# Products that nobody reads, placed on the matrix engine in seven idle stretches of a fused two-layer decoder

## Chip, cores and metric

The kernel runs on one core of a Trainium2 chip. The metric is the time on the device in microseconds, from one launch of the whole program. Lower is better. The engines are called PE (TensorE, PEld for its weight loads), DVE (VectorE), ACT (ScalarE), POOL (GpSimd) and SP (the queue that issues the DMAs).

## What is computed

Two decoder layers on `x` of 16 sequences x 128 positions x 128 features. Each of the six sublayers is added to `x`, and each reads a layer norm of it; the program counts the layer norms from 0, the text from the first.

```python
x = x + mamba(layernorm(x))                    # 1st norm: W_in, delta, B, C, a scan over 128 positions, W_out
x = x + cross_attention(layernorm(x), ctx)     # 2nd norm: one head, 120 context rows of 64
x = x + experts(layernorm(x))                  # 3rd norm: 8 experts, top 2, and a shared one
x = x + reflected_lru(layernorm(x))            # 4th norm: the recurrence below
x = x + heads_attention(layernorm(x), ctx)     # 5th norm: 16 heads of 8
x = x + selu_experts(layernorm(x))             # 6th norm: 8 experts, top 2, hidden 512

def step(h_prev, x_t, v_t, lam_t):             # of reflected_lru, 127 times
    Qh = h_prev - 2.0 * v_t * (sum(v_t * h_prev) / sum(v_t * v_t))
    return lam_t * Qh + (1.0 - lam_t) * x_t
```

All experts are computed for all positions and weighed afterwards, so the shapes are fixed.

## The kernel before

It is written engine by engine: each engine has one program, and semaphores named in `S` order them. The 16 sequences are handled in four groups (`NG` = 4) of four (`GB` = 4), so most products have 128 x 512 outputs, one bank of PSUM. TensorE takes its instructions strictly in the order of its program, so a wait in it holds back all that stands behind. `bank(n)` is PSUM bank n, and `mm` is a matrix product; `mm(out, ident, y)` copies y.

A layer norm for group g goes round the engines. VectorE computes the statistics (L812 to L818), GpSimd the inverse deviation (L319, L320), ScalarE normalizes the first two sequences (L507, semaphore `ln_xn_a`) and VectorE the other two (L824, `ln_xn_b`). TensorE transposes the four (`transpose_xn`, L1338), ScalarE copies them out of PSUM (`copy_xnT`, L510 to L518, semaphore `ln_xnT`), and VectorE keeps what is lost in the shorter type (`ln_lower`, L827 to L834, `ln_lo`). The projections behind it are `up` (L1352, three products for one output, line L1356) and `down` (L1345, line L1349).

The places that the change touches, in order of time:

- The first norm and `W_in`. TensorE waits for `const`, set by GpSimd when the identity is built (L327 to L329), transposes group 0, then per group transposes the next one and makes four `up` outputs. ScalarE applies silu to them (L544); before that it loads a table.
- The fourth norm: three transposed groups, then `xz(0)` (12 products of L1356), the fourth group, `xz(1)`, and the products with `Wl` and `Wv` (L1569).
- `chunk_dots` and `solve`: TensorE's dot products in groups, with which VectorE solves for chunks of four positions (`u_done`, `c_done`, L1100 to L1122). The third and the fourth group's `solve` come after TensorE's last dot product.
- The rounds: 32 chunks (`NC`) one after the other. A round is a chain between VectorE (L1183 to L1199) and TensorE: `s_known` (L1629) puts known sums in PSUM, and a product with ones (L1639) adds what depends on the last round. In each round but the last stand two products with the identity into bank 5 that nobody reads (L1643). VectorE handles finished spans between (`piece`, L1143).
- After the last round VectorE, ScalarE and GpSimd finish the last span and the gate (`gated`), and TensorE waits for it and makes the output projection with `down`.
- The fifth norm: TensorE makes the keys of all groups (L1653), then per group the transposes (L1342) and the values (L1659, which wait for VectorE's `hk_lo`), then the queries (L1664) with a bias row of 128 x 128 (L1666). ScalarE takes them in the order normalize, key copy, copy of the group before, value copy of the group before (`keys_and_values`, L589).
- The attention with 16 heads: a loop over 16 sequences. `head_scores` (L1675, on 32 rows each), `head_transposes` (L1685), `head_values` (L1696), `head_sums` (L1704), `head_out` (L1710) on TensorE. VectorE takes the maximum and subtracts it (L1233, L1236) and divides (L1241), ScalarE takes exponentials and copies (L766, L771), GpSimd spreads keys and values (L460, L477). The first scores stand ahead of a wait for all queries (`hq_lo`).

Of the kernel before, what the change touches and what calls it, by code (L numbers as in the profile page):

```python
# [12 lines left out]
P = 128  # L13
B, T, D = 16, 128, 128
N = B * T
GB = 4
NG = B // GB
# [29 lines left out]
def decoder_program(nc, a, out):  # L47

    with ExitStack() as ctx:
# [1285 lines left out]
        def _(pe):  # L1335
            mm = nc.tensor.matmul

            def transpose_xn(i, g):  # L1338
                for b in range(GB):
                    if b % (GB // 2) == 0:  # L1340
                        pe.wait_ge(S["ln_xn_b" if b else "ln_xn_a"], i * NG + g + 1)
                    ins = nc.tensor.transpose(bank(ln_bank(i, g))[:, 0, b * T:(b + 1) * T], xn[:, g * GB + b, :], ident[:])  # L1342
                ins.then_inc(S["ln_tr"], 1)
# [15 lines left out]
            pe.wait_ge(S["const"], 1)  # L1359

            transpose_xn(0, 0)
            for g in range(NG):
                if g + 1 < NG:
                    transpose_xn(0, g + 1)
                pe.wait_ge(S["w_split"], 1)
                pe.wait_ge(S["ln_lo"], g + 1)
                for m in range(4):
                    if g:
                        pe.wait_ge(S["in_silu"], 4 * g - 3 + m)
                    up(bank(4 + m)[:, 0, :], 0, m, g).then_inc(S["in_mm"], 1)  # L1370
# [177 lines left out]

            for g in range(NG - 1):
                transpose_xn(3, g)  # L1550
            pe.wait_ge(S["w_lru"], 16 * 6)
# [74 lines left out]
            def s_known(c):  # L1626
                if c >= 2:
                    pe.wait_ge(S["s_copied"], c - 1)
                mm(slot(c), ident[:], cp.rearrange("p (q k) -> p q k", k=KG)[:, :, GB * c:GB * c + GB], start=True, stop=False,  # L1629
                   skip_group_check=True)  # L1630

            pe.wait_ge(S["vv_read"], NG)
            pe.wait_ge(S["l_ev"], HI * NG)
# [3 lines left out]
            for c in range(NC):  # L1637
                pe.wait_ge(S["r_sum"], c + 1)
                mm(slot(c), ones[:], us[:, c % 2], start=False, stop=True, skip_group_check=True).then_inc(S["s_mm"], 1)  # L1639
                if c + 1 < NC:  # L1640
                    s_known(c + 1)
                    for k in range(2):
                        mm(bank(5)[:, 0, 0:256], ident[:], cp[:, 0:256], start=True, stop=True)  # L1643
            pe.wait_ge(S["z_silu"], 2 * HI)
            pe.wait_ge(S["s_copied"], NC)
# [9 lines left out]
            for g in range(NG):  # L1655
                transpose_xn(4, g)
                pe.wait_ge(S["hk_lo"], g + 1)
                for b in range(GB):
                    ins = mm(bank(4 + g)[0:LK, 0, b * D:(b + 1) * D], w["ctxT"][:, g * GB + b, :], w["Wv1"][:], start=True, stop=True)  # L1659
                ins.then_inc(S["hv_mm"], 1)  # L1660
            for g in range(NG):
                pe.wait_ge(S["hv_ev"], g + 1)
# [51 lines left out]
            head_scores(0, 1)  # L1714
            pe.wait_ge(S["hq_lo"], NG)
            for b in range(B + 2):
                if b + 1 < B:
# [123 lines left out]
```

## Time and profile before

| | |
|---|---|
| median of 3 runs | 1047.51 us (1047.32 to 1052.38) |
| the profiled execution, whole | 1046.03 us |
| its span, first to last instruction | 1044.3 us |
| mean granted clock of TensorE | 0.958 |
| PE / PEld busy | 903.1 / 665.5 us (86% / 64%) |
| DVE / ACT / POOL busy | 811.1 / 544.6 / 420.2 us |
| chain that ended last | PE 52%, DVE 17%, ACT 5%, issue 3%, POOL 1% |

The granted clock is a share of TensorE's full 2.4 GHz; it has two levels here, 1.00 and 0.50. The first record of it stands at 15.4 us, and the views print 1.00 ahead of it, where nothing was recorded. Shares of busy time are means over stages with different limits, so a stage is read by its own rows. In a row of the timeline stand: start, length, engine and line, operation, tiles, shapes, count, and in brackets how long the engine was idle before it and what released it. A row may merge several instructions, and its length then reaches from the first to the last. A few records of matrix products can be missing.

### The profile page before, as it was taken

How to read it: one execution, taken by the hardware profiler on the slowest of the kernel's cores; microseconds unless marked ns; L12 is line 12 of the kernel's file. 1: busy time of each engine (PE TensorE's matmuls, PEld its weight loads, DVE VectorE, ACT ScalarE, POOL GpSimd, SP SyncE). 2: the span in 40 equal slices, each digit the busy share in tenths (PEclk: the TensorE clock that was granted, in tenths of full speed). 3: DMA queues.
4: the chain of work that ended last, by engine and by line, in shares of the span. 5: the costliest groups of instructions: out<-in, count | busy, mean ns of one | idle time of the engine just before them, and what ended most of it. 6: DMA issues, size and time to landing. Idle time of an engine off the chain costs nothing.

```text
span 1044.3 us, 15167 instructions
## 1 busy us (share of the span) xinstructions
PE 903.1 (86%) x5628; PEld 665.5 (64%) x5628; DVE 811.1 (78%) x1450; ACT 544.6 (52%) x979; POOL 420.2 (40%) x400
## 2 busy tenths in 40 slices
PE   6967877778899999989885767899968999999997
PEld 4432222223688888866654546576646789999997
DVE  6799999999767555573897886599975588878886
ACT  6456566654653222236533223466645467677775
POOL 6479999999200101112982354544420001011110
PEclk9979999999999999999987997599999999999999
DMA  6000000000001001000000001000000000000001
GB/s 186 1 0 1 0 1 0 0 1 1 1 2 31 16 16 31 16 1 1 1 0 1 1 1 41 1 2 2 2 1 1 1 21 21 6 16 21 21 21 41
DMA packets 19860, 13.82 MB, mean 13 GB/s; under 512 B 3067, under 2 KB 18313, under 8 KB 19786
## 3 DMA queue, kind: packets, MB, share of 16 engines
q1 hardware_dynamic: 19786, 12.84, 4.4%
q8 instruction: 45, 0.74, 0.3%
q14 instruction: 29, 0.24, 0.1%
HBM read 11.79 MB, written 1.05 MB: 12 GB/s over the span
## 4 chain that ended last, share of the span: by engine, by line
PE 52%; DVE 17%; ACT 5%; issue 3%; POOL 1%; DVEq 0%; ACTq 0%; POOLq 0%
PE ps L1356 19%; PE ps L1349 17%; PE ps L1569 3%; DVE small L1233 2%; PE ps L1743 2%; DVE G L1236 2%; PE ps L1685 1%; PE ps L1639 1%; PE ps L1400 1%; DVE R L1194 1%; DVE stats L812 1%; DVE ps L1199 1%; PE ps L1675 1%; DVE ps L1183 1%; DVE R L1185 1%
## 5 line engine op out<-in xcount | busy, mean ns | idle before, releaser
L1356 PE MATMUL ps<-xhl,whl 128*128 128x512 f32 x960 | 247.3, 407 | 12.7 <-DVE xhl L834 5.1
L1356 PEld LDWEIGHTS ps<-xhl,whl 128*128 128x128 f32 x960 | 179.1, 194 | 52.3 <-issue 13.4
L784 ACT ACTIVATE G<-ps,w_exp_bi 128x512 f32<-128x512 f32 x128 | 89.9, 702 | 65.9 <-PE ps L1356 54.9
L1349 PEld LDWEIGHTS ps<-R,G 128*128 128x128 f32 x1024 | 119.0, 192 | 6.4 <-DVE G L1279 4.1
L1349 PE MATMUL ps<-R,G 128*128 128x128 f32 x1024 | 119.7, 275 | 3.1 <-DVE G L1279 3.1
L356 POOL TENSOR_TENSOR R<-G,R 128x1024 f32<-128x1024 f32 x43 | 100.5, 2352 | 19.4 <-ACT R L550 15.8
L942 DVE TENSOR_TENSOR_SCAN R<-ps,R 128x1024 f32<-128x1024 f32 x43 | 97.6, 2279 | 5.7 <-POOL R L365 5.7
L785 ACT ACTIVATE G<-ps,ebs 128x512 f32<-128x512 f32 x144 | 102.0, 708 | 0.0
L649 ACT ACTIVATE G<-ps 128x512 f32<-128x512 f32 x72 | 42.8, 597 | 112.8 <-PE ps L1356 112.8
L1039 DVE SCALAR_TENSOR_TENSOR X<-ps,cw,X 128x128 f32<-128x128 f32 x272 | 76.5, 344 | 23.4 <-PE ps L1349 23.2
L1279 DVE SCALAR_TENSOR_TENSOR G<-G 128x1024 f32<-128x1024 f32 x72 | 91.6, 1272 | 2.5
L1278 DVE TENSOR_SCALAR G<-G 128x1024 f32<-128x1024 f32 x72 | 55.2, 767 | 47.6 <-ACT G L785 47.2
L1379 PE MATMUL ps<-bc,sel 96*128 96x512 bf16 x128 | 46.8, 394 | 49.8 <-ACT LN L557 22.1
L324 POOL CAST whl<-R 128x512 fp32r<-128x512 f32 x8 | 6.5, 819 | 195.0 <-DMA R<-in_exp_wo_dram 162.8
L577 ACT ACTIVATE ps<-G,negA 128x508 f32<-128x508 f32 x128 | 83.3, 689 | 3.0 <-DVE R L942 2.9
L1048 DVE TENSOR_TENSOR G<-G,ps 128x512 f32<-128x512 f32 x72 | 49.0, 687 | 44.5 <-ACT G L649 44.5
L1400 PE MATMUL ps<-R,ident 128*128 128x512 f32 x172 | 82.0, 599 | 0.0
L550 ACT COPY R<-ps 128x512 f32<-128x512 f32 x64 | 37.4, 585 | 77.7 <-PE ps L1379 77.7
L1379 PEld LDWEIGHTS ps<-bc,sel 96*128 96x128 bf16 x128 | 12.5, 98 | 102.3 <-ACT LN L557 35.8
L1349 PEld LDWEIGHTS ps<-ew,G 128*128 128x128 f32 x576 | 69.6, 191 | 2.8 <-DVE G L1048 0.3
L1349 PE MATMUL ps<-ew,G 128*128 128x128 f32 x576 | 70.2, 275 | 0.1
L319 POOL TENSOR_TENSOR rstd<-small,mhalf 128x4 f32<-128x4 f32 x24 | 24.7, 1028 | 83.9 <-DVE small L818 83.9
(270 smaller groups left out, 1726.2 us busy)
## 6 DMA issues: line engine op xcount, KB each, us to landing
ew<-in_w_dram SPq DMA_DIRECT2D x24, 128.0 KB, 2.2
R<-in_exp_wi_dram SPq DMA_DIRECT2D x8, 256.0 KB, 2.7
R<-in_exp_wo_dram SPq DMA_DIRECT2D x8, 256.0 KB, 3.2
X<-in_x_dram SPq DMA_DIRECT2D x4, 256.0 KB, 3.9
out_dram<-X SPq DMA_DIRECT2D x4, 256.0 KB, 2.3
w_ctxT<-in_ctxT_dram SPq DMA_DIRECT2D x1, 487.5 KB
ew<-in_sw_dram SPq DMA_DIRECT2D x3, 128.0 KB, 2.5
w_W_in<-in_W_in_dram SPq DMA_DIRECT2D x1, 256.0 KB, 3.0
```

The lines of the kernel that those rows point to most:

```text
L356: gp.tensor_tensor(halves(dBu[i % 3]), duT[:, :, gcols(i // NS)], Bsb[:, i % 4:i % 4 + 1, :].broadcast_to([P, HI, GT]), ALU.mult).then_inc ...
L577: sc.activation(bank(2 * j + m)[:, 0, :].rearrange("p (b t) -> p b t", b=GB)[:, :, 1:T], dT[:, m, gcols(g)].rearrange("p (b t) -> p b t", ...
L784: sc.activation(G[:, 0, slot, m * GT:(m + 1) * GT], banks[:, m, :], ACT.Exp, bias=exp_bias[m])
L785: sc.activation(G[:, 1, slot, m * GT:(m + 1) * GT], banks[:, m, :], ACT.Relu, bias=lin_bias[m], scale=SELU_L).then_inc(S[act_s], 1)
L942: v.tensor_tensor_scan(hst[i % 3], bank(2 * j, 2).rearrange("p h n -> p (h n)"), dBu[i % 3], 0.0, ALU.mult, ALU.add).then_inc(S["scanned"], 1)
L1039: ins = v.scalar_tensor_tensor(X[:, bi, :], bank(4 + i % 2)[:, 0, b * D:(b + 1) * D], cw[:, bi, e:e + 1], X[:, bi, :], ALU.mult, ALU.add)
L1278: step(v.tensor_scalar(G[:, 0, slot, half], G[:, 0, slot, half], 1.0, 1.0, ALU.min, ALU.subtract))
L1279: ins = v.scalar_tensor_tensor(G[:, 2, slot, half], G[:, 0, slot, half], SELU_LA, G[:, 1, slot, half], ALU.mult, ALU.add)
L1349: ins = mm(bank(o)[:, 0, b * width:(b + 1) * width], lhs(k, b), rhs(k), start=k == 0, stop=k == ks - 1)
L1356: ins = mm(mix(out) if n == N_WIN1 else out, whl[:, wslot(n), i, m * P:(m + 1) * P], rhs, start=k == 0, stop=k == 2)
L1379: mm(bank(bank_i)[:, 0, :], sel[:, r, :], bc3[:, gcols(g)], start=True, stop=True).then_inc(S[s], 1)
L1400: ins = mm(bank(6 + m)[:, 0, :], ident[:], hC[i % 3][:, m * GT:(m + 1) * GT], start=False, stop=i % NS == NS - 1, skip_group_check=True)
```

## The change

TensorE's program gets a helper, `unread(o, n)`: n products of the identity with itself, 128 x 128 in float32, into the first quarter of PSUM bank o. Nobody reads them, and no semaphore is set by them. 115 of them are placed: 18, 5 and 3 in the first norm; 5, 3 and 7 in the fourth; 14 ahead of the rounds; 34 behind them; 6 behind the values of each of the first three groups in the fifth norm; 8 behind the first scores of the attention. The 14 stand behind three new waits (for all but the last group's `solve` and copy), because bank 5 is in use till then; the 6 stand behind a new wait for the copy of group 0, because bank 0 holds its transposes. No other engine's program changes.

```diff
+            def unread(o, n):
+
+                for _ in range(n):
+                    mm(bank(o)[:, 0, 0:P], ident[:], ident[:], start=True, stop=True)
+
-            def transpose_xn(i, g):
+            def transpose_xn(i, g, between=0):
                 for b in range(GB):
+                    if b == GB // 2:
+                        unread(7, between)
                     if b % (GB // 2) == 0:
                         pe.wait_ge(S["ln_xn_b" if b else "ln_xn_a"], i * NG + g + 1)
...
             pe.wait_ge(S["const"], 1)
 
+            unread(7, 18)
             transpose_xn(0, 0)
+            unread(7, 5)
             for g in range(NG):
                 if g + 1 < NG:
                     transpose_xn(0, g + 1)
+                if g == 0:
+                    unread(7, 3)
...
-            for g in range(NG - 1):
-                transpose_xn(3, g)
+            transpose_xn(3, 0)
+            transpose_xn(3, 1)
+            unread(7, 5)
+            transpose_xn(3, 2, between=3)
+            unread(7, 7)
...
+            pe.wait_ge(S["u_done"], 3 * (NG - 1))
+            pe.wait_ge(S["c_done"], 2 * (NG - 1))
+            pe.wait_ge(S["e_ev"], NG - 1)
+            unread(5, 14)
             pe.wait_ge(S["vv_read"], NG)
...
+            unread(5, 34)
             pe.wait_ge(S["z_silu"], 2 * HI)
             pe.wait_ge(S["s_copied"], NC)
...
                 ins.then_inc(S["hv_mm"], 1)
+                if g + 1 < NG:
+                    pe.wait_ge(S["ln_xnT"], 4 * NG + 1)
+                    unread(0, 6)
...
             head_scores(0, 0)
             head_scores(0, 1)
             pe.wait_ge(S["hq_lo"], NG)
+            unread(7, 8)
```

## Rows read from the trace of the kernel before

**Rows 1.** The page, TensorE's granted clock in 40 equal slices, in tenths.
```profile
PEclk9979999999999999999987997599999999999999
```

**Rows 2.** Stretches: start and end, length, busy time of five engines, clock, DMA.
```profile
465.90:472.70 6.80, 5.40 (x13) 4.17 (x14) 2.34 (x5) 2.67 (x6) 0.00 (x0) 0.50 0.00 1
...
551.30:564.90 13.60, 6.69 (x23) 5.82 (x23) 10.16 (x29) 4.07 (x10) 0.00 (x0) 0.50 0.00 0
...
565.00:623.00 58.00, 45.17 (x229) 32.03 (x228) 48.93 (x168) 14.61 (x64) 24.41 (x30) 1.00 0.00 1
...
632.30:636.50 4.20, 4.19 (x19) 4.20 (x20) 0.40 (x1) 0.00 (x0) 0.00 (x0) 0.50 0.00 0
636.70:650.20 13.50, 12.09 (x86) 9.87 (x85) 12.18 (x55) 6.91 (x16) 6.16 (x14) 1.00 0.29 80
650.30:660.40 10.10, 10.10 (x26) 5.99 (x26) 2.16 (x3) 4.52 (x9) 5.71 (x3) 0.50 0.00 0
660.60:663.80 3.20, 1.43 (x14) 0.52 (x12) 2.60 (x4) 2.05 (x3) 3.20 (x8) 1.00 0.00 0
663.90:677.50 13.60, 12.39 (x76) 8.88 (x78) 10.10 (x9) 5.93 (x9) 4.78 (x12) 0.50 0.00 1
677.70:765.00 87.30, 80.82 (x1263) 60.61 (x1260) 81.48 (x125) 54.32 (x84) 37.02 (x84) 1.00 0.01 2
```

**Rows 3.** The timeline at the start, all engines.
```profile
1.41 0.29 POOL L329 TENSOR_SCALAR_AFFINE_SELECT ident<-ident 128x128 f32<-128x128 f32 x1 [0.24 <-POOL ident L328]
...
9.29 0.56 ACT L518 CAST xhl<-ps 128x512 fp32r<-128x512 f32 x1
...
10.89 5.07 PE L1356 MATMUL ps<-xhl,whl 128*128 128x512 f32 x12 [0.34 <-DVE xhl L834]
...
14.90 1.28 ACT L544 ACT_TABLE_LOAD   x1
```

**Rows 4.** The chain that ended last: start, length, engine and line, count.
```profile
452.15 1.78 PE ps L1349 x16
...
467.30 5.46 PE ps L1356 x12
473.27 2.74 PE ps L1356 x12
...
632.31 3.77 PE ps L1349 x16
```

**Rows 5.** The timeline in the fourth norm and around the rounds.
```profile
463.64 0.44 PE L1342 MATMUL ps<-ident,LN 128*128 128x128 f32 x2 [1.36 <-ACT LN L507]
...
464.98 0.44 PE L1342 MATMUL ps<-ident,LN 128*128 128x128 f32 x2 [0.90 <-DVE LN L824]
...
552.11 0.28 DVE L1122 TENSOR_TENSOR R<-R,ps 128x128 f32<-128x128 f32 x1
...
558.00 0.66 PE L1629 MATMUL ps<-R,ident 128*128 128x64 f32 x2 [9.74 <-DVE R L1122]
...
623.14 0.43 PE L1639 MATMUL ps<-R,ones 128*128 128x64 f32 x2 [0.46 <-DVE R L1185]
```

**Rows 6.** VectorE's timeline in the rounds, one instruction of each.
```profile
558.73 0.20 DVE L1188 TENSOR_TENSOR R<-LN,ps 128x32 f32<-128x32 f32 x1
...
566.07 0.20 DVE L1188 TENSOR_TENSOR R<-LN,ps 128x32 f32<-128x32 f32 x1
568.03 0.20 DVE L1188 TENSOR_TENSOR R<-LN,ps 128x32 f32<-128x32 f32 x1
```

**Rows 7.** The timeline of the queries in the fifth norm.
```profile
653.61 1.92 PE L1664 MATMUL ps<-LN,w_Wq 128*128 128x512 f32 x2
...
656.17 4.98 PE L1664 MATMUL ps<-LN,w_Wq 128*128 128x512 f32 x6
```

**Rows 8.** What VectorE waited for from 661 to 684 us: in total, times, longest.
```profile
DVE G L1241 <- PE ps L1704: 3.4, 1, 3.4
DVE small L1233 <- PE ps L1675: 1.8, 2, 1.2
```

## The prediction

> **What bounds the kernel now.** I read the slices of the page first, for TensorE's granted clock: in most of the span it is full, and it dips in slices 3, 21, 22, 25 and 26 [rows 1]. Then the table of stretches, cut where the clock changes. The reader is to see five long stretches at 0.50, which is 1.2 of the 2.4 GHz, and what TensorE did in and before them [rows 2]: 465.9 to 472.7 us (fourth layer norm), 551.3 to 564.9 (into the rounds), 632.3 to 636.5 (output projection behind the rounds), 650.3 to 660.4 and 663.9 to 677.5 (fifth layer norm, first turns of attention). In the last one TensorE is busy for 12.39 of 13.6 us, so there it works at half speed and others wait for it. Third, the chain that ended last, for the price: twelve `up` products take 5.46 us at the low clock and 2.74 at the full one, sixteen instructions of `down` 3.77 against 1.78 [rows 4]. All four low pieces that the sum uses lie on that chain. So the kernel is bound by TensorE or VectorE by turns, and a few microseconds are lost wherever TensorE comes back from a pause.
>
> **Price of one product.** A plain float32 product is recorded as two MATMULs: `down` with four batches and two halves is eight products and stands as x16 [rows 4]. With 128 columns one MATMUL is 1.78/16 = 0.111 us at full clock and 3.77/16 = 0.236 at the low one, so a product is 0.22 or 0.47 us. The change adds 115 of them, 230 MATMULs, 25.6 us at full clock. Nothing reads them; they cost only where they still run when the next needed instruction is ready.
>
> **Start (26 products).** TensorE may begin when the identity is built, at 1.41 + 0.29 = 1.7 us [rows 3]. The clock is low there: twelve `up` products take 5.07 us at 10.89 [rows 3], like the 5.46 above, though no fall is printed. 36 MATMULs at 0.236 would end at 10.2. But dense work raises the clock: it rose 4.3 us after 632.3, and 5.5 after 467.3 [rows 2, 4]. Here that is 6.0 to 7.2 us; by then 18 to 23 are done and the rest take 2.0 to 1.4 us, so they end near 8.0 to 8.6. With the four transposes (0.111 us each) behind them that is 8.5 to 9.1, and ScalarE, busy till then, takes the copy that reads them only at 9.29 [rows 3]. The next 5 and 3 products (1.1 and 0.7 us) fit between the groups at full clock. Does the faster first projection pay? It ends about 2.3 us sooner, but ScalarE's table load ends at 14.90 + 1.28 = 16.2 [rows 3] and the silus that release the next group wait for that. So I take 0. Bounds: a gain of 0.3 if ScalarE's order loosens, and 1.2 lost if the longer pause before 16.9 lets the clock fall again under the second group (half of its 2.7 us, more than ScalarE can hide).
>
> **Fourth layer norm (5, 3 and 7).** Between the transposes and the projection the engine pauses; the last one is released by VectorE's split, and the projection starts at 467.30 [rows 4]. The products are 1.1, 0.7 and 1.6 us; the gaps that they stand in are 1.36 us ahead of the third group's first half and 0.90 ahead of its second, then 467.30 - 465.42 = 1.88 ahead of the projection [rows 4, 5]. All fit at full clock, and it is full until 465.9 [rows 2]. With them the engine is busy for most of these 5 us, so the clock should stay up: 5.46 - 2.74 = 2.7 us gained [rows 4]. Next behind it is TensorE's own second projection, so the gain goes through. Bounds 0 and 2.9.
>
> **Before the rounds (14).** The new waits (third group solved) end with the `c_done` instruction at 552.11 + 0.28 = 552.4 [rows 5]; they are weaker than the waits behind them, so nothing else is held. TensorE has by then been idle since 558.00 - 9.74 = 548.3 and the clock is low from 551.3 [rows 2, 5]. 28 MATMULs at 0.236 are 6.6 us, to 559.0, against the first needed product at 558.00 [rows 5]; with the rise 4.3 to 5.5 us after their start they end at 557.7 to 558.5. So they hold the start back by 0 to 0.5 us (1.0 at worst), but the rounds run at full clock from the first. The first three rounds took 566.07 - 558.73 = 7.34 us, the next 1.96 [rows 6]: 7.34 - 3 x 1.96 = 1.46. I take 1.2 gained; bounds 1.0 lost and 1.5 gained.
>
> **After the rounds (34).** TensorE ends its last needed product at 623.14 + 0.43 = 623.6 [rows 5] at full clock, and `down` starts at 632.31 [rows 4]: a gap of 8.7 us. 68 x 0.111 = 7.5 us, to 631.1. The margin is 1.2 us, ten MATMULs at the low clock. Then the first group of `down` takes 1.78 instead of 3.77 us, and VectorE's residual and statistics wait for exactly that group: 2.0 gained, bounds 7.3 lost (see the rivals) and 2.3 gained.
>
> **Fifth layer norm (3 x 6).** Each call waits for ScalarE's copy of the first group and then runs 12 MATMULs, 1.3 us. Behind them on the queue stand the next transposes and values products, for which ScalarE waits. Together 4.0 us; in 636.7 to 650.2 TensorE is idle for 13.50 - 12.09 = 1.4 [rows 2], so the work is pushed 2.6 us later. The low clock of 650.3 to 653.6 gives back half of 3.3, so the queries start 0.9 late. They (with the bias row) took from 653.61 to 656.17 + 4.98 = 661.15 [rows 7], 7.5 us at the low clock, and at the full one half: 3.8. Net 2.8 earlier. Bounds: 2.6 lost if the clock stays low here, 3.5 gained.
>
> **Attention's first turn (8).** 16 MATMULs, 1.8 us, wait for VectorE's last lower part of the queries, with which a pause opens: TensorE was busy for 1.43 of 3.2 us in 660.6 to 663.8 [rows 2]. They fill the pause and no more. Between 661 and 684 VectorE waits 3.4 and 1.8 us for TensorE's sums and scores [rows 8]. In 677.7 to 765 VectorE is busy for 81.48 of 87.3 us [rows 2], so it sets the pace once the clock is up, and what is gained at the entry stays. These 5.2 us go at full clock; I take 4.7, since small waits remain. Bounds 0 and 5.7.
> The rule that speaks against this place: the first turns consist of transposes and of scores on 32 rows. In 677.7 to 765 the turns consist of them too, with values and sums between, and the clock is 1.00; but in 663.9 to 677.5 it stayed at 0.50 although TensorE was busy nine tenths of the time [rows 2]. The Trainium skill, TensorE: Matmul & The Clock Gate, Part 4: PE-mode transpose, says that a transpose doesn't count as busy in the way that other matmuls do. By it the sum would be 4.7 us smaller, since the clock would fall again behind the eight products; it is a rival below.
>
> **Sum.** 0 + 2.7 + 1.2 + 2.0 + 2.8 + 4.7 = 13.4 us. The profiled execution took 1046.0 us (span 1044.3 and 1.7 around it), so it would be 1032.6. The median of the runs is 1047.5, 1.5 above; against it 1034.1. I predict 1034. Where the clock falls will differ between executions by a few microseconds (the three runs reach from 1047.3 to 1052.4), so single dips may move.
>
> **The rivals.**
> 1. The clock falls again in attention's first turns. For it: the 663.9 row, the narrow scores. Against: TensorE is full-clock in all later turns, made of the same instructions, and eight full-width products stand right ahead. It gives 1034 + 4.7 = 1039. Chance 0.20.
> 2. The dips only move, or what is gained in the layer norms is given back behind the added wait of the fifth one and at the start (2.6 and 1.2 lost, no gain in the queries and attention): 1047.5 - 2.7 - 1.2 - 2.0 + 2.6 + 1.2 = 1045. For it: 4.0 us of products stand ahead of needed transposes there. Chance 0.09.
> 3. Slower: the 34 products run at the low clock. If a product of the identity with itself holds the clock no better than a pause, the clock falls a few us into the gap. All 68 at 0.236 are 16.0 us against a gap of 8.7, 7.3 late; more than ten at the low clock are enough for a loss. The fifth layer norm's 36 MATMULs at 0.236 are 8.5 us against 1.4 of idle, 7.1 more. No gain is left, and this gives 1047.5 + 7.3 + 7.1 = 1062. Against: the spare products of the rounds also multiply by the identity, and with them the clock is 1.00 through 565 to 623, where TensorE is busy for 45.17 of 58 us [rows 2]. Chance 0.04.
> 4. The products do all that is said in the layer norms and after the rounds, but VectorE absorbs less than I think in attention and half of that gain goes: 1034 + 2.4 = 1036. It lies in the forecast's own range.
>
> **How the numbers follow.** Forecast 0.67 (1030 to 1038, with rival 4), rival 1 0.20 (1037 to 1041), rival 2 0.09, rival 3 0.04. The range from 1030 to 1042 holds the first two and a little of rival 2. A measurement of this kernel can tell about 0.5% from no change, which is 1042.3 and 1052.7. Faster by more: 0.67 + 0.20 + 0.01 = 0.88; within: 0.08; slower: 0.04.
>
> **What would show it.** In the profile after: `up` at the fourth layer norm's end near 2.75 us; three first rounds at 1.96 each; the first sixteen `down` MATMULs at 1.8 us and starting when the gate releases them, not later; the queries' eight MATMULs at 3.4 us; VectorE's waits for sums and scores in the first turns gone; no clock of 0.50 between 558 and 765. The mean granted clock should go from 0.958 to about 0.98. Wrong would be a `down` that starts behind the spare products, transposes of the first layer norm's first group that end after 9.3 us, or a low clock under attention's first turns.

## The result and the profile after

The changed kernel took 1035.14 us (median of 4 runs, 1033.03 to 1037.51) against 1048.04 for the kernel before (4 runs, 1047.32 to 1052.38): ratio 0.9858, 95% interval 0.983 to 0.9885. On the chip of the last experiments it took 1038.83 (6 runs) against 1048.38: 0.9909, 0.9889 to 0.9929. Both belong to the result; of the 3.7 us between them the profiles show 2.3, which the experiments trace to one place, and the rest is open. Every ratio in this document is against the kernel before on the same chip in the same set of runs, and leaves out one execution of 3184.89 us, at a clock of 1.00, of the kernel with 68 products below, which no trace explains.

| | before | after |
|---|---|---|
| profiled execution, whole | 1046.03 us | 1035.33 us |
| its span | 1044.3 us | 1033.6 us |
| mean granted clock | 0.958 | 0.975 |
| TensorE busy, instructions | 903.1 us | 917.7 us, x5858 |

The clock in 40 slices of the span, to be held against [rows 1]:

```profile
PEclk9989999999999999999988999999998999999999
```

Slices 21 and 22 still dip, and so does slice 31, but the deep dips of 25 and 26 are gone. The table of stretches of after, in the columns of [rows 2], cut where its own clock changes:

```profile
18.40:21.80 3.40, 3.40 (x9) 2.65 (x9) 0.93 (x3) 2.75 (x6) 3.25 (x2) 0.50 0.81 240
467.10:470.10 3.00, 2.96 (x14) 2.44 (x15) 0.98 (x2) 1.76 (x3) 0.00 (x0) 1.00 0.01 3
486.10:489.50 3.40, 3.40 (x5) 1.34 (x5) 3.30 (x4) 1.87 (x4) 3.04 (x3) 0.50 0.00 0
499.70:503.10 3.40, 3.40 (x11) 2.29 (x10) 3.22 (x3) 1.65 (x4) 3.32 (x5) 0.50 0.00 0
550.90:557.70 6.80, 5.38 (x25) 5.41 (x26) 6.51 (x14) 3.40 (x6) 0.12 (x1) 0.50 0.00 0
...
630.70:645.00 14.30, 14.30 (x106) 12.46 (x107) 11.48 (x54) 5.56 (x12) 5.37 (x9) 1.00 0.25 74
650.50:656.30 5.80, 5.16 (x25) 2.14 (x23) 3.01 (x5) 4.28 (x7) 3.91 (x1) 1.00 0.00 0
656.30:667.50 11.20, 9.85 (x104) 7.43 (x108) 11.03 (x10) 6.88 (x11) 8.24 (x20) 1.00 0.01 1
```

From 557.8 to 772.7 us no clock of 0.50 is left. But there are three falls that the kernel before did not have, at 18.4, 486.1 and 499.7 us, and in the sixth norm a second one at 779.6. Now TensorE's timeline at the places of the products (L1341 is the spare product; L1349 the transposes, L1356 `down`, L1363 `up`, L1686 the queries, L1697 the scores):

```profile
1.76 5.71 PE L1341 MATMUL ps<-ident 128*128 128x128 f32 x36 [1.76 <-POOL ident L329]
7.77 0.44 PE L1349 MATMUL ps<-ident,LN 128*128 128x128 f32 x2 [0.29 <-ACT LN L507]
8.93 0.44 PE L1349 MATMUL ps<-ident,LN 128*128 128x128 f32 x2 [0.72 <-DVE LN L824]
...
18.24 4.57 PE L1363 MATMUL ps<-xhl,whl 128*128 128x512 f32 x12 [2.63 <-ACT G L544]
...
465.08 1.73 PE L1341 MATMUL ps<-ident 128*128 128x128 f32 x14
467.14 2.99 PE L1363 MATMUL ps<-xhl,whl 128*128 128x512 f32 x12 [0.33 <-DVE xhl L832]
...
552.32 5.95 PE L1341 MATMUL ps<-ident 128*128 128x128 f32 x28 [4.21 <-DVE G L1120]
558.10 0.33 PE L1643 MATMUL ps<-R,ident 128*128 128x64 f32 x2
...
621.78 7.81 PE L1341 MATMUL ps<-ident 128*128 128x128 f32 x68
...
650.58 1.02 PE L1686 MATMUL ps<-LN,w_Wq 128*128 128x512 f32 x2
...
651.94 2.84 PE L1686 MATMUL ps<-LN,w_Wq 128*128 128x512 f32 x6
...
656.35 2.05 PE L1341 MATMUL ps<-ident 128*128 128x128 f32 x16 [0.69 <-DVE qhl L1225]
658.96 0.92 PE L1697 MATMUL ps<-kz,qhl 32*128 32x480 f32 x6 [0.56 <-POOL kz L460]
```

The 68 MATMULs behind the rounds take 7.81 us and end at 629.6, a microsecond ahead of `down`. The six last of the queries take 2.84 us against 4.98 in [rows 7]. What VectorE waits for from 648 to 671 us, for [rows 8]:

```profile
DVE qhl L1225 <- ACT qhl L757: 5.0, 1, 5.0
DVE G L1241 <- PE ps L1726: 0.8, 1, 0.8
```

The 3.4 and 1.8 us for sums and scores have become 0.8. Next behind TensorE at this place is GpSimd, which spreads keys and values. These pieces of the chain that ended last, between the queries and the first turn, are now its:

```profile
652.39 4.53 POOL X L470
656.92 1.90 POOL kz L460 x2
658.83 0.14 issue
658.96 0.92 PE ps L1697 x6
```

The two profiles are compared by the start of the same VectorE instruction at the end of each stage. Each number is microseconds gained in the stage (minus: lost). "The rest" is what lies between the first scan and 464 us, and behind 679 us. The last column is a second profile of the same changed kernel, taken with the last experiments.

| stage, up to | predicted | after | after, again |
|---|---|---|---|
| start, to the first scan (56 us) | 0 | 0.28 | -2.01 |
| fourth norm, to its last split (474 us) | 2.7 | 2.5 | 2.5 |
| its recurrence, to the first round (559 us) | 0 | -2.5 | -2.4 |
| entry to the rounds (566 us) | 1.2 | 1.45 | 1.44 |
| behind the rounds, fifth norm, queries (662 us) | 2.0 + 2.8 | 4.75 | 4.74 |
| attention's first turn (679 us) | 4.7 | 4.57 | 4.55 |
| the rest | 0 | -0.3 | -0.3 |
| sum | 13.4 | 10.7 | 8.4 |

In the first profile five of the stages with a price came out within 0.3 us. What is missing is the fourth norm's gain, given back in the stage behind it, and in the second profile 2 us at the start.

### The profile page after: what moved, and what is told of

The parts are those of the page before. It is cut to its first block, busy times and chain, and to the rows that moved or that the text cites. A ratio compares the mean times of both kernels' runs of the same rounds, so it can differ in the third digit from the quotient of the medians.

```text
span 1033.6 us, 15627 instructions
## 1 busy us (share of the span) xinstructions
PE 917.7 (89%) x5858; PEld 683.8 (66%) x5858; DVE 806.5 (78%) x1450; ACT 545.2 (53%) x979; POOL 419.5 (41%) x400
## 4 chain that ended last, share of the span: by engine, by line
PE 54%; DVE 15%; ACT 4%; issue 3%; POOL 2%; DVEq 0%; ACTq 0%; POOLq 0%
PE ps L1363 20%; PE ps L1356 18%; PE ps L1583 3%; DVE small L1233 2%; PE ps L1766 2%; DVE G L1236 2%; PE ps L1411 1%; PE ps L1657 1%; DVE R L1194 1%; PE ps L1707 1%; DVE ps L1199 1%; DVE ps L1183 1%; DVE R L1185 1%; PE ps L1697 1%; DVE stats L812 1%
## 5 line engine op out<-in xcount | busy, mean ns | idle before, releaser
L1363 PE MATMUL ps<-xhl,whl 128*128 128x512 f32 x960 | 245.9, 406 | 12.6 <-DVE xhl L834 4.8
L1363 PEld LDWEIGHTS ps<-xhl,whl 128*128 128x128 f32 x960 | 178.7, 193 | 50.9 <-issue 14.3
L1356 PEld LDWEIGHTS ps<-R,G 128*128 128x128 f32 x1024 | 119.0, 192 | 6.4 <-DVE G L1279 4.1
L1356 PE MATMUL ps<-R,G 128*128 128x128 f32 x1024 | 119.7, 275 | 3.1 <-DVE G L1279 3.1
L356 POOL TENSOR_TENSOR R<-G,R 128x1024 f32<-128x1024 f32 x43 | 101.7, 2382 | 17.5 <-ACT R L550 17.1
L1356 PEld LDWEIGHTS ps<-ew,G 128*128 128x128 f32 x576 | 69.6, 191 | 2.8 <-DVE G L1048 0.3
L1356 PE MATMUL ps<-ew,G 128*128 128x128 f32 x576 | 70.2, 275 | 0.1
L319 POOL TENSOR_TENSOR rstd<-small,mhalf 128x4 f32<-128x4 f32 x24 | 24.7, 1029 | 83.5 <-DVE small L818 83.5
```

The source lines that it names most:

```text
L356: gp.tensor_tensor(halves(dBu[i % 3]), duT[:, :, gcols(i // NS)], Bsb[:, i % 4:i % 4 + 1, :].broadcast_to([P, HI, GT]), ALU.mult).then_inc ...
L1356: ins = mm(bank(o)[:, 0, b * width:(b + 1) * width], lhs(k, b), rhs(k), start=k == 0, stop=k == ks - 1)
L1363: ins = mm(mix(out) if n == N_WIN1 else out, whl[:, wslot(n), i, m * P:(m + 1) * P], rhs, start=k == 0, stop=k == 2)
```

## The experiments

Differences are against the profile of before, at the same VectorE instructions; "+" is later. Each profiled kernel shows one execution, so where a fall of the clock is put down to an edit, it is said how many profiles bear it out. The kernel before took 1050.61 us in the median beside the first four experiments (18 runs, 1045.74 to 1055.31), 1049.13 beside the next four (13 runs), 1048.38 beside the three after those and 1048.19 beside the last. Its own mean granted clock goes from 0.946 in the executions of 1054 to 1055 us to 0.96 in that of 1045.76, so a ratio just below 1, as in the first two experiments, may come from where the clock fell in the kernel before; there the profile is the better guide.

**The fourth norm alone.** All products left out but these:

```diff
             transpose_xn(3, 1)
+            unread(7, 5)
+            transpose_xn(3, 2, between=3)
+            unread(7, 7)
```

> Only the 15 products of the fourth layer norm. The question is why the 2.5 us that the first projection gained there were gone 50 us later. Theory: no engine is saturated, the clock fell at two new places (486.1 and 499.7 us) under needed products. Then VectorE's split of the fourth group comes 2.5 us sooner than before here too, and how much of it is left at 517 us depends on where the clock falls between: all of it (1045.0 against 1047.7 before) if it doesn't fall there more than before, nothing (1047.7) if it falls twice more; the trace shows each microsecond under a low clock. Rival: VectorE or ScalarE is the bound from there on; then nothing is left at 517 us whatever the clock does (1047.7), and VectorE has no more idle time than before.

Measured 1047.45 us, ratio 0.9966 (0.994 to 0.9991). In its profile the first split of the fourth norm is at +0.57 and the last at -1.94: 2.5 gained there. At the third group's reciprocal (517 us) it is +0.84: all given back, and the kernel ends at +0.55, so its 1047.45 us is no gain over the 1047.5 of before. The rows show how:

```profile
486.62 5.30 PE L1579 MATMUL ps<-G,w_Wl 128*128 128x512 f32 x8
491.75 3.60 PE L1579 MATMUL ps<-G,w_Wv 128*128 128x512 f32 x8
```

The eight `Wl` MATMULs take 5.30 us where the same number with `Wv` takes 3.60, since the clock is low from 487.0 to 490.4 and again from 500.7 to 504.1, as in the changed kernel 0.9 us earlier.

**Around the rounds alone.** Only the 14 and the 34:

```diff
+            unread(5, 14)
             pe.wait_ge(S["vv_read"], NG)
...
+            unread(5, 34)
             pe.wait_ge(S["z_silu"], 2 * HI)
```

> Only the 14 and the 34 around the rounds. By the sum of the prediction: the first three rounds at 1.96 us each (1.45 gained), the first sixteen instructions of the output projection in 1.8 us instead of 3.8 (2.0 gained): 3.4 us less, 1044.3. With the engine at full clock when the fifth norm begins, but no products there, the clock falls again in it as before: the low stretches at 650 and 664 stay. Rival (the two gains are taken back by the fifth norm's own pauses): under 1 us less, 1047.

Measured 1046.96, 0.9963 (0.9939 to 0.9987). From +2.08 at the first round to +0.65 at the fourth: 1.43 gained. `down` takes 7.38 us, and 9.46 in the kernel of the next experiment, which has no 34: 2.08. At the queries' copy the kernel stands at -0.90, 1.55 gained. Then the clock is low from 649.0 to 659.2 and from 666.0 to 679.7, as before the change, so the attention gains nothing. Both prices of the prediction stand. The kernel ends at +0.78: 1.6 us are lost at a fall at 297 us, 0.7 in the attention and 1.2 in the sixth norm with falls at 782 and 792 us, all under instructions that its edit doesn't touch. So the 1044.3 of the theory was missed, and the time is the rival's 1047, but not for the rival's reason: at 637 us, behind the projection, the kernel is at -1.09, and at 662, behind the queries, at -1.11, so the fifth norm took nothing back.

**The fifth norm and the eight alone.**

```diff
+                if g + 1 < NG:
+                    pe.wait_ge(S["ln_xnT"], 4 * NG + 1)
+                    unread(0, 6)
...
+            unread(7, 8)
```

> Only the 3 x 6 of the fifth norm and the 8 of the attention. By the sum: 2.8 + 4.7 = 7.5 us less, 1040.2, with the projection behind the rounds still in 3.8 us and the rounds as before. Rival (the full clock in the fifth norm needs the 34 ahead of it): the clock still rises in the projection, as it did before at 636.6 us, so it can't be needed; if it were, the queries would stay at 5 us for six instructions and the gain would be under 3 us, 1045.

Measured 1040.99, 0.9893 (0.9854 to 0.9932). From +1.87 behind the rounds to -5.47 at the first division of attention: 7.3 us. `down` still runs at the low clock, 628.3 to 638.5 us, and then none is low until 778.5. So the two edits don't need the 34, and they carry most of what the change brings.

**The changed kernel without the eight.**

```diff
-            unread(7, 8)
```

> The changed kernel without the 8 products ahead of the attention's loop. Theory A: the 8 hold the clock through the pause of some 2 us; without them it falls at about 657 to 661 us, the first turns run at half speed, and 4.7 us are lost: 1039.8. Theory B: the fifth norm enters at full clock and the pause alone doesn't end it: no fall, within 0.5 us of the changed kernel, 1035. Before the change the clock fell there with 1.4 us of work in the 3.2 us ahead of the fall; I give A 0.65.

Measured 1040.88, 0.9899 (0.9854 to 0.9943). Against the changed kernel it is 2.5 us late ahead of the first turn and 6.3 behind it: 3.8 of the 4.6 hang on these eight products. Theory A holds, with the fall at 662.8 us. Its timeline there, where TensorE waits 3.31 us for GpSimd, and the stretch behind it:

```profile
661.46 0.91 PE L1697 MATMUL ps<-kz,qhl 32*128 32x480 f32 x6 [3.31 <-POOL kz L460]
662.30 1.55 PE L1707 MATMUL ps<-ident,G 128*120 128x128 f32 x8
...
670.68 1.96 PE L1707 MATMUL ps<-ident,G 128*120 128x128 f32 x8
```

```profile
662.90:672.90 10.00, 9.92 (x67) 7.01 (x67) 7.16 (x7) 4.95 (x8) 4.08 (x11) 0.50 0.01 2
```

Eight transposes take 1.96 us and not 1.09, with TensorE busy all the time: its lateness is now the others' wait.

**Transposes in place of products.** Twice as many, so that the time is the same (a transpose is one MATMUL):

```diff
-                for _ in range(n):
-                    mm(bank(o)[:, 0, 0:P], ident[:], ident[:], start=True, stop=True)
+                for _ in range(2 * n if tr else n):
+                    if tr:
+                        nc.tensor.transpose(bank(o)[:, 0, 0:P], ident[:], ident[:])
...
+            unread(5, 34, tr=True)
...
+                    unread(0, 6, tr=True)
...
+            unread(7, 8, tr=True)
```

> The changed kernel, with the unread products behind the rounds, in the fifth norm and ahead of the attention's loop made transposes of the identity, two for each product, so that each MATMUL recorded in its place stays one MATMUL of 128 columns. Theory 1 (a transpose counts for the clock as a product does): as the changed kernel, full clock from 557 to 770 us, first sixteen instructions of the output projection in 1.8 us, 1035. Theory 2 (the Trainium skill, TensorE: Matmul & The Clock Gate, Part 4: a transpose doesn't count as busy in the same way): the clock falls some 3 to 7 us after the last round, the first sixteen take 3.8 us, the transposes run at 0.236 us each and end after the gate (68 in up to 12 us against 8.9), and the fifth norm and the first turns run at half speed: 1047 or more.

Measured 1038.68, 0.9901 (0.9869 to 0.9932). The rows behind its rounds, and its stretch from the rounds to the end of attention:

```profile
624.27 7.59 PE L1342 MATMUL ps<-ident 128*128 128x128 f32 x68
633.18 1.02 PE L1359 MATMUL ps<-w_Wout,R 128*128 128x128 f32 x7 [1.31 <-POOL R L435]
```

```profile
559.30:774.20 214.90, 181.96 (x2023) 138.21 (x2021) 181.69 (x424) 100.48 (x210) 90.38 (x165) 1.00 0.02 6
```

The clock is 1.00 throughout, and the distance to the changed kernel is 2.5 us ahead of the rounds and 2.4 behind attention. So transposes hold a clock that is up as the products do; whether they also raise a low one, no run shows. The Trainium skill, TensorE: Matmul & The Clock Gate, Part 4: PE-mode transpose, says that they don't count as busy in the same way; as far as holding the clock goes, these rows don't agree with it.

**Sixty-eight for thirty-four.**

```diff
-            unread(5, 34)
+            unread(5, 68)
```

> The changed kernel with 68 instead of 34 products behind the rounds. All theories agree that they run at full clock, 136 x 0.111 = 15.1 us from 621.8 on, so the output projection starts at 636.9 instead of 630.7: 6.2 us later. If TensorE's queue sets the end there, all of it is seen at the end: 1035 + 6.2 = 1041.3. If the fifth norm or the attention takes up a part, less; I give full 0.85. It is the price of products that outlast their pause.

Measured 1044.75, 0.9947 (0.9928 to 0.9965). The 136 MATMULs take 15.40 us, and `down` starts at 639.85, directly behind them:

```profile
624.61 15.40 PE L1341 MATMUL ps<-ident 128*128 128x128 f32 x136
639.85 7.31 PE L1356 MATMUL ps<-w_Wout,R 128*128 128x128 f32 x64
```

Against the changed kernel it is 2.8 us late ahead of them and 9.1 behind: 6.3, which it keeps to attention's end. With the 1.1 us that were free ahead of `down` that is 7.4 us for 34 more products, so one that no longer fits costs its full 0.22 us. The 2.8 us ahead of them are 2.0 from the start, 3.3 from a fall at 308 us and 2.5 less because the fourth norm's gain is kept; both come up next.

**Products in the recurrence too.** The changed kernel with seven ahead of the sums of v squared of the two last groups, and two behind those of each:

```diff
+                pe.wait_ge(S["l_ev"], HI * (g + 1))
+                if g >= 2:
+                    unread(1, 7)
                 v_dot_v(g)
+                unread(1, 2)
                 spread_reciprocal(g)
```

> The changed kernel plus products in the stage between the fourth norm and the rounds, where the 2.7 us of the fourth norm were lost again: 7 products (1.55 us) in the pause of 1.9 us ahead of the third and the fourth group's sums of squares, and 2 (0.44 us, against 0.28 us of idle) between the sums of squares and the spread reciprocals of each group. Theory: the loss was by new falls of the clock under needed products (486 and 500 us), so with these there is no fall between 466 and 548, the group's spread reciprocals take 1.2 us in all four groups, and of the 2.7 us at least 2 are still there at 558 us: 1035 - 2 - up to 1.5 for the falls at 517 and 534 that were there before = 1032 to 1033. Rival: VectorE is the bound in that stage; then the falls go and the time stays at 1035, with more waiting of TensorE for VectorE.

Measured 1034.64, 0.9858 (0.981 to 0.9905). Its four executions reach from 1029.46 to 1038.30 us, and the profiled one took 1037.55. The falls at 486 and 500 us are gone in it, and so is that at 534: against the changed kernel it goes from +5.1 at the fourth norm's last split to +1.9 at the first round. I took this for the work of the products added here. It was not: the kernels without the eight, with the 68 and (below) without the start have no such products, and they hold the fourth norm's gain as well (at 474 and 517 us: +2.5 and +2.5, +2.7 and +2.7, +3.0 and +3.0). Their own part is 0.6 us in this profile: at the first round this kernel is at +1.7, and the one without the eight at +2.3. All three, and this one, have another fall instead, in the third norm's experts:

```profile
305.44 4.53 PE L1526 MATMUL ps<-w_router,LN 128*128 128x8 f32 x32
309.82 3.76 PE L1356 MATMUL ps<-ew,G 128*128 128x128 f32 x16
313.24 3.74 PE L1363 MATMUL ps<-xhl,whl 128*128 128x512 f32 x12
```

The clock is low from 308.0 to 314.8. It falls 2.6 us after the start of the 32 products with 8 columns each, and it costs 3.3 us (+1.6 to +4.9 from 296 to 458 us).

**The sixth norm's pause filled, the start empty.** As the last, without the 26 at the start, and with

```diff
             for g in range(NG - 1):
                 transpose_xn(5, g)
+            pe.wait_ge(S["hs_sub"], 2 * B)
+            unread(0, 16)
```

> As the run with products in the stage ahead of the rounds, without the 26 at the start, and with 16 products (3.6 us) in the 4.8 us pause of the sixth norm ahead of the gate's projection. Theory: the 26 at the start bring nothing, since ScalarE's table load sets when the silus begin, and cost 1.6 us when the clock falls in the longer pause that they leave ahead of the second group; without them the second group's projection takes 3.0 us as before. The sixth norm: twelve products in 2.75 instead of 4.6 us, 1.8 gained, and no fall at 779. Together 1029 to 1032. Rival (the 26 do shorten the start): the first silu of the third group comes later than in the changed kernel.

Measured 1032.92, 0.9843 (0.981 to 0.9876).

```profile
767.51 3.74 PE L1341 MATMUL ps<-ident 128*128 128x128 f32 x32
772.48 3.01 PE L1363 MATMUL ps<-xhl,whl 128*128 128x512 f32 x12 [1.23 <-DVE xhl L834]
```

`up` takes 3.01 us here and 4.58 in the changed kernel: 1.5 us gained over the sixth norm, and kept to the end. Of the two falls of the changed kernel there (772.8 to 776.2 and 779.6 to 786.4) one is left, from 780.0 to 783.4, so "no fall at 779" was wrong. ScalarE's silus of the third group in the first projection begin at 21.44 and not at 23.98 us (the first silu at 16.52 and not at 17.50), so the rival is wrong too. The fall near 308 is there again (305.6 to 312.4).

**The router's products in two halves.** As the last, with the 32 narrow products split:

```diff
-            def router_logits():
+            def router_logits(half):
...
-                for b in range(B):
+                for b in range(half * B // 2, (half + 1) * B // 2):
...
+                if half:
+                    ins.then_inc(S["rt_mm"], 1)
...
                 if i == 2:
-                    router_logits()
+                    router_logits(0)
...
                          lambda k: ew0[:, sl, 2, k * D:(k + 1) * D], 4 + c % 2).then_inc(S["down0"], 1)
+                if i == 2:
+                    router_logits(1)
```

> The version with the 26 products at the start left out, with products also beside the fourth norm's recurrence and in the sixth norm's pause, and now with the router's 32 narrow products (128x8) of both batches no longer in one piece: half before, half behind one of the down-projections of the third norm's stage. Theory (the narrow products are what the clock falls behind at 305 to 315 us, though they keep TensorE busy): the fall there goes, some 3.3 us with it, and the time is 1029 to 1030. Rival 1: the place of that fall only varies from kernel to kernel, and has nothing to do with the narrow products: a fall near 308 stays or turns up within 20 us of it, 1033 as without the split. Rival 2: the later half holds up whoever reads the logits, 1 to 2 us lost between 305 and 350 us, at the full clock.

Measured 1032.08, 0.9837 (0.9815 to 0.9858).

```profile
306.14 1.85 PE L1522 MATMUL ps<-w_router,LN 128*128 128x8 f32 x16
307.84 2.03 PE L1356 MATMUL ps<-ew,G 128*128 128x128 f32 x16
309.71 1.85 PE L1522 MATMUL ps<-w_router,LN 128*128 128x8 f32 x16
311.42 2.98 PE L1363 MATMUL ps<-xhl,whl 128*128 128x512 f32 x12
```

```profile
300.00:320.00 20.00, 20.00 (x138) 18.27 (x137) 9.12 (x23) 7.90 (x12) 0.00 (x0) 1.00 0.00 1
```

The fall at 308 is gone, at no cost for who reads the logits: +2.4 at 296 and at 458 us, where the kernel without the start has +2.3 and +5.5 with the same instructions up to 300 us. The time is not the 1029 to 1030 of the theory: against the kernel of the last experiment, on which that rests, this profile loses 3 us from 49 to 56 us, which comes next. It is also the slowest of the five executions, which reach from 1030.01 to 1033.56.

**The changed kernel again, and without its start.** The first has no edit, the second:

```diff
-            unread(7, 18)
             transpose_xn(0, 0)
-            unread(7, 5)
...
-                if g == 0:
-                    unread(7, 3)
```

> The changed kernel itself, beside the others of this call, without an edit: for its time on the same chip, and for which of its clock falls stand where they stood. Expected: 1035 by both theories. If the falls at 486, 500, 517, 534 and 551 us stand within 1 us of where they stood, the stage behind the fourth norm gives the gain back in every execution; if one of them is gone or another has come at 305 to 315 us, part of what was put down to edits of the third norm's stage is only what one execution happens to do (some 1.5 to 3.3 us each).

> The changed kernel without the 26 products at the start (18, 5 and 3), all else as changed. Theory: they buy nothing, since the first projection stands behind its loads, and they cost the fall at 18 to 22 us: the first norm's weights come 1 to 2.9 us earlier, and this is absorbed or kept by the recurrence at 50 to 56 us; the time is 1034 to 1035.5, at most 1.3 under the changed kernel on the same chip. Rival: the products do keep the clock up for the second group, and without them the projections of 18 to 25 us run at half the clock as before: L544's last instruction at 24 us or later, and a time 1 us or more over the changed kernel.

Measured 1038.83, 0.9909 (0.9889 to 0.9929), and 1038.81, 0.9902 (0.988 to 0.9924). The changed kernel's profile has every fall from 290 us on where it was, 2.3 us later. The falls at 486 and 500 are among them:

```profile
488.30:491.70 3.40, 3.40 (x6) 1.34 (x5) 3.29 (x4) 1.87 (x3) 2.97 (x3) 0.50 0.00 0
502.00:505.30 3.30, 3.30 (x11) 2.31 (x10) 3.09 (x3) 1.63 (x4) 3.22 (x5) 0.50 0.00 0
```

The 2.3 us arise from 51 to 58 us: at VectorE's last L912 ahead of the first scan this profile is 0.85 us early, and at the scan 2.3 late. 2.2 come from the instruction itself, and 0.9 from a wait for TensorE behind it. In VectorE's timeline the first row is of the first profile of after, the second of this one:

```profile
51.82 1.22 DVE L912 TENSOR_TENSOR G<-G 128x1024 f32<-128x1024 f32 x1
```

```profile
50.97 3.42 DVE L912 TENSOR_TENSOR G<-G 128x1024 f32<-128x1024 f32 x1
```

Beside it GpSimd changes from one L356 to the next at 51.81 us in the first and 50.96 in the second. In the first, VectorE's takes 1.22 and GpSimd's 3.44; in the second GpSimd's 2.35 and VectorE's 3.42. They start within 10 ns of each other, and one of them has to wait, for about as long as the other takes alone: VectorE 2.2 us or GpSimd 1.1. That is what the Trainium skill, SBUF — State Buffer, under "SBUF: two separate sides", says of the pair of ports that VectorE and GpSimd share: an exclusive lock, held for the whole instruction, which blocks the other. The trace agrees. VectorE won in two of the fourteen profiles (the first of after, and the sixth norm's kernel), GpSimd in twelve.

With this taken out, the products at the start can be priced: both profiles have 3.42 there, and the first scan is at 57.76 with them and at 56.19 without, 1.6 us lost. ScalarE's silus of the third group begin at 23.14 and 21.55: with the products the clock fell at 17.3 us, under the second group's projection. Without the start the kernel does not come out faster, since its profile has the fall at 308 (308.6 to 315.4, 3.2 us) that this one lacks, and keeps the fourth norm's gain, which this one gives back. My 1034 to 1035.5 for it was wrong, and "at most 1.3 under the changed kernel on the same chip" was right.

**Without the recurrence's products.** The router's kernel less the two edits in the recurrence:

```diff
-                pe.wait_ge(S["l_ev"], HI * (g + 1))
-                if g >= 2:
-                    unread(1, 7)
                 v_dot_v(g)
-                unread(1, 2)
```

> The version with the router's products in two halves, without the 26 at the start, with the sixteen in the sixth norm, and now without the products beside the fourth norm's recurrence (seven ahead of two of its groups, two in each). Theory (the recurrence's products have nothing to do with it: with the same instructions the clock fell at 486 and 500 us in the three profiles that had no fall at 308, and in none of those that had one or had the router's products split): no fall between 475 and 515 us, the fourth norm's 2.5 us are kept at 517, and the time is that of the version with them, 1032 within 1. Rival: the products beside the recurrence held the clock there: falls near 488 and 502 return, 2.5 us are given back by 519, and the time is 1034 to 1035.

Measured 1034.6 (6 runs, 1030.94 to 1036.63), 0.9862 (0.9832 to 0.9892); the median is outside the 1 us that I gave, the two intervals overlap, and the runs of both scatter over 3.5 and 5.7 us. The profiles can be compared row by row: at the ends of all stages the two agree within 0.15 us, up to the last instruction. There is no fall between 480 and 517 us:

```profile
480.00:517.00 37.00, 33.77 (x143) 21.72 (x141) 27.21 (x33) 24.73 (x35) 26.93 (x30) 1.00 0.00 1
```

So in this profile the fourth norm's gain stays without the recurrence's products. What they change is the length of the fall at 534 us, 3.4 us with them and 6.9 without, and at 545 us the two kernels are level within 0.05 us. What they do in other executions is not shown: the mean granted clock of the router's kernel is 0.983 to 0.985 in the four executions that were not profiled and 0.98 in the profiled one, and here it is 0.977 to 0.979 in five of six and 0.985 in the fastest.

## Why the prediction was right and where it failed

The time was right: 1034 forecast, 1035.14 measured, faster by more than 0.5% in both measurements. On the second chip, too, 1038.83 lies within the range of 1030 to 1042.

- **The price of one product** held. 68 MATMULs take 7.81 us, 0.115 each, against 0.111; doubled, each costs that.
- **Start.** The spare MATMULs end at 7.5 us in the first profile and at 8.5 in the second (8.0 to 8.6 said), the first group's transposes at 9.4 and 9.0 (8.5 to 9.1 said). The 9.4 is past the 9.3 that I had named as a sign of being wrong, but it isn't the spare products that hold them: the last two wait 0.72 us for VectorE's norm, which had waited 1.40 us for the load of `x`, against 0.70 in the second profile. The step that failed is the choice of 0 within its own bounds. The reason named for the lower bound is what happened: the pause ahead of the second group is 2.63 us with the products and 0.5 to 0.9 without, and the clock falls under that group. It costs 1.6, more than the 1.2 of the bound. It isn't certain either: the kernel with transposes has the same start, and there no fall came (12 MATMULs in 3.01 us, the first scan at 55.60). In the first profile the loss was hidden because VectorE's L912 took 2.2 us less and a wait behind it 0.9. The second profile of the same kernel has neither, so the 0.28 that fits my 0 is luck.
- **Fourth layer norm.** 2.5 gained for 2.7, in all the profiles looked at (after twice, alone, without the start). The step that failed is "Next behind it is TensorE's own second projection, so the gain goes through". Instructions further on started earlier, and the clock fell under them at 486 and 500 us where it had not before. What I left out is that the clock's state later on changes as well when work moves. It is not a property of the stage alone: three profiles with these products gave the gain back (after twice, alone), seven kept it to 517 us (without the eight, with 68, the two with the recurrence's nine and the start in or out, the split router with and without them, without the start), and that with transposes lost part of it by a fall at 501. None of the three had a fall at 308, and five of the seven had one, so the sum over both is about the same.
- **Before the rounds** 1.45 for 1.2. The needed product starts at 558.10 and stood at 558.00: 0.1 late, in the 0 to 0.5 given.
- **After the rounds** 2.08 for 2.0 on `down`, by the two kernels with and without the 34. The margin of the gap was there, and with 68 the mechanism of rival 3 is seen, though at the full clock.
- **Fifth layer norm.** Without what came before, the queries start 0.7 late (0.9 said). With bias they take 4.2 us (650.58 to 651.94 + 2.84) for 7.5; 3.8 was said. Net 2.7 for 2.8.
- **Attention's first turn** 4.57 for 4.7, 3.8 of it by the eight. Rival 1, the fall in the first turns, did not come, and the kernel with transposes takes its reason away. What is late next is GpSimd, which I had not named.
- **Rival 2** was half right: a dip did move and a gain was given back, but in the fourth norm's stage and not in the fifth, where I looked for it. Rival 4 is excluded by the 4.57, of which nothing is lost up to the end of attention.

Which fall comes, the one at 308 or those at 486 and 500, is not the same for the same instructions: up to the router's products eight of the kernels have the same (the one before, the first three experiments, and the four of the later ones that leave out the start). In the profiles it goes with where the work stands against a fall before it. Every profile has one that starts between 285 and 298 us. Where the router's first product starts 15.3 to 15.6 us behind that start (the kernel before, the changed one twice, the fourth norm alone) or 8.4 behind it (the other two with only a part of the products), there is no fall at 308. Where it starts 14.2 to 14.8 us behind it (without the eight, transposes, 68, with the recurrence's) there is one.

The four that leave out the start stand at 17.7 to 17.9: with the router's products in one piece the clock fell and 3.2 and 3.3 us were lost, with them in halves it didn't, twice, and nothing was lost. So in this position the split is what took the fall away, as far as two profiles against two can show it. What stays open is how often an execution stands so. Nor was it tried whether another order of the two engines at 51 us saves the 2.2 us always.

The version with the lowest median is that with the split router, with products in the recurrence and in the sixth norm's pause, without the start: 1032.08 us, 0.9837 of before (0.9815 to 0.9858), where the changed kernel has 0.9909 on the same chip. Its lead over the version without the split (0.9843, 0.981 to 0.9876) lies within the intervals.

## What to carry to other kernels

Spare products pay where a stage is entered from a pause and TensorE is late in that stage: price them by the row of one MATMUL, end them ahead of the next released instruction, and look there for what is late next. Count the gain only at the far end of the next stages, since an earlier start also changes where the clock falls later on; a gain of 2.5 us was given back this way. For differences of a few microseconds take more than one profile of the same kernel: two of the changed kernel differ by 2.2 us in a single instruction.

## What the hardware did that I had not expected

- The clock also fell where TensorE stood as busy. In six profiles it fell 2.3 to 2.8 us after the start of the router's 32 MATMULs of 8 columns (4.2 to 4.7 us busy), at 306 to 309 us, with no pause ahead. In the fourth norm's recurrence, 16 MATMULs of one column stand ahead of each of the falls at 486 and 500. They stand there in every kernel, the one before too, in which no fall follows, so they alone don't bring it. Here in the timeline of after:

```profile
482.80 1.84 PE L1593 MATMUL ps<-ones,LN 128*128 128x1 f32 x16
484.92 1.16 PE L1599 MATMUL ps<-ident,rvv 128*128 128x128 f32 x8 [0.28 <-DVE rvv L1128]
485.91 5.29 PE L1583 MATMUL ps<-G,w_Wl 128*128 128x512 f32 x8
```

- Where the clock falls under unchanged instructions differs from kernel to kernel, by up to 3.3 us in a stage. From 290 us on it repeated itself between two profiles of the changed kernel, one of which ran 2.3 us later; but its falls came 2.2 us later as well, so the work stood against them as before, and the pair doesn't test another position. Other executions of one kernel differ: the kernel before took 1045.74 to 1055.31 us at mean clocks of 0.96 to 0.946.
- Transposes of the identity held a clock that was up as products do: 68 of them for 7.59 us, and 12 and 16 at a time later, in a stretch of 214.9 us at 1.00.
- VectorE and GpSimd, started within 10 ns of each other, keep one of them waiting, VectorE 2.2 us or GpSimd 1.1. Which one it is differed between two executions of one kernel, and where it was VectorE, the next stage began 2.2 us later.
